# A latent-attention kernel: its preparation merged into one block, part of it beside the norms, and the steps behind its main loop re-ordered

## What is computed

```python
h = layernorm(layernorm(x)) * ln_scale + ln_bias        # the norms of two layers in a row
c_q, c_kv = h @ w_down_q.T, h @ w_down_kv.T             # 128 -> 64 each
q = rope(c_q @ w_up_q.T); k = rope(c_kv @ w_up_k.T)     # 16 heads of 64
v = c_kv @ w_up_v.T                                     # folded with w_out per head
attn = softmax(q @ k.T / 8)                             # 2048 x 2048 for each head
out = (attn @ v) @ w_out.T + 2 * x                      # the input comes in twice: here and around the layer
```

## Time and profile before

| | |
|---|---|
| median of 3 executions | 2093.56 us |
| the profiled execution's own time | 2090.94 us |
| its span, first to last instruction | 2089.1 us |
| PE busy over the span | 1881.3 us (90%) |
| DVE, ACT, POOL busy | 1605.3, 1259.2, 1076.7 us |
| mean granted TensorE clock | 0.950 of full speed |

### The profile page before, as it was taken

The page is one execution under the profiler, slowest core; times in us unless marked ns, Lnnn a source line. Parts: engine busy times, 40 slices in busy tenths (PEclk is TensorE's granted clock), DMA queues, the critical chain, the costliest instruction groups (busy, mean ns, idle before and its releaser), DMA issues. The chain is left out here.

```text
span 2089.1 us, 36118 instructions
## 1 busy us (share of the span) xinstructions
PE 1881.3 (90%) x11422; PEld 937.2 (45%) x11422; DVE 1605.3 (77%) x2448; ACT 1259.2 (60%) x2593; POOL 1076.7 (52%) x1225
## 2 busy tenths in 40 slices
PE   5755898989865999999999999999999999999598
PEld 2542486547642444444344443444443444444346
DVE  6787776676655788888888888788888888888265
ACT  6533685468520677777677777677776677777231
POOL 0735743574205466566566566566565566566200
PEclk9987899989976999999999999999999999999699
DMA  1001021002015699998898988899998889999243
GB/s 37 1 1 68 22 59 32 6 17 64 14 57 203 242 324 339 334 330 324 319 339 323 352 323 326 319 327 330 341 336 320 315 317 330 341 329 334 79 105 80
DMA packets 201467, 452.16 MB, mean 216 GB/s; under 512 B 12048, under 2 KB 159248, under 8 KB 200240
## 3 DMA queue, kind: packets, MB, share of 16 engines
q1 hardware_dynamic: 201264, 449.67, 60.9%
HBM read 228.77 MB, written 206.83 MB: 209 GB/s over the span
## 5 line engine op out<-in xcount | busy, mean ns | idle before, releaser
L1602 ACT ACTIVATE g.probs<-g_score,g.lowest 128x1024 f32<-128x1024 f32 x514 | 567.9, 1109 | 328.9 <-DVE g.lowest L1588 328.9
L1588 DVE TENSOR_REDUCE g.lowest<-g_score 128x1 f32<-128x1024 f32 x514 | 605.5, 1219 | 184.1 <-PE g_score L1556 184.1
L1556 PE MATMUL g_score<-g.keys,g.queries 64*128 64x512 f32 x2056 | 500.4, 605 | 20.5 <-PEq L1474 10.7
L1688 DVE STREAM_TRANSPOSE g.blocks<-g.probs 128x768 f32<-128x768 f32 x512 | 467.1, 950 | 1.0
L1618 PE MATMUL g_mix_ps<-g.far,mid.y_tok 128*64 128x512 f32 x1584 | 382.9, 605 | 0.0
L1556 PEld LDWEIGHTS g_score<-g.keys,g.queries 64*128 64x128 f32 x2056 | 183.7, 187 | 250.5 <-ACT g.probs L1602 130.8
L1648 POOL TENSOR_TENSOR g.scaled<-g.scaled,g.coef 128x1024 f32<-128x1024 f32 x67 | 127.0, 1896 | 247.8 <-ACT g.scaled L1640 240.0
L1708 POOL TENSOR_TENSOR mid.y_tok<-mid.y_tok,g.waves 128x512 f32<-128x512 f32 x128 | 162.3, 1268 | 76.0 <-ACT mid.y_tok L1571 76.0
L1461 POOL TENSOR_TENSOR g.queries<-mid.y_tok 64x256 f32<-64x256 f32 x256 | 185.4, 724 | 19.6
L1578 PEld LDWEIGHTS g_turned<-top.ident,g.probs 128*128 128x128 f32 x1024 | 107.6, 141 | 194.7 <-issue 194.7
L1578 PE MATMUL g_turned<-top.ident,g.probs 128*128 128x128 f32 x1024 | 168.4, 287 | 0.0
(11 more groups left out here) (369 smaller groups left out, 2778.7 us busy)
## 6 DMA issues: line engine op xcount, KB each, us to landing
g.far<-bounce SPq DMA_DIRECT2D x257, 768.0 KB, 7.0
bounce<-g.blocks SPq DMA_DIRECT2D x256, 768.0 KB, 6.2
e.share<-shares SPq DMA_DIRECT2D x8, 1024.0 KB, 16.9
g.far<-g.near SPq DMA_DIRECT2D x7, 768.0 KB, 6.7
lt0.v_late<-la0.v SPq DMA_DIRECT2D x6, 512.0 KB, 10.1
lt1.v_late<-la1.v SPq DMA_DIRECT2D x6, 512.0 KB, 9.4
bounce<-g.near SPq DMA_DIRECT2D x4, 768.0 KB, 9.4
top.upto<-stored_mixers SPq DMA_DIRECT2D x33, 64.0 KB, 6.5
```

Source lines behind the costliest of these rows:

```text
L1556: nc.tensor.matmul(score[:, 2 * pair + odd], queries[rows, turn, head, cols], keys[rows, turn, head, pair * CH:(pair + 1) * CH], start=Tru ...
L1588: nc.vector.tensor_reduce(lowest[:, unit, half, r:r + 1], score[:, 2 * half:2 * half + 2].rearrange("p b n -> p (b n)"), AX.X, ALU.max, ne ...
L1602: nc.scalar.activation(probs[:, r % 2, half * 2 * CH:(half + 1) * 2 * CH], score[:, 2 * half:2 * half + 2].rearrange("p b n -> p (b n)"), ...
L1688: ins = nc.vector.transpose(blocks[:, r, :, REST * half:REST * (half + 1)].rearrange("p j t c -> p t j c"), probs[:, r % 2, at:at + REST * ...
```

## The change

- `normalise_twice` now runs inside `latent_attention`, and its SP and POOL streams get work. SP issues all the loads of blocks 2 and 3, clears the retired semaphores, and, once POOL has zeroed `near`, issues the 11 fills of 768 KB. POOL does all the memsets.
- Blocks 2 and 3 become one. Small weights and the transposed tokens `hT` lie in unused halves of `queries`. ACT takes the transposed tokens, the lowered tokens and the values out of PSUM; scale, bias and factor ride on ACT's copy. PE computes the mixers first, then interleaves transposes, `lower` and the projections of the first chunks, with the values between the second and the third chunk.
- The rotary sums are split: DVE adds the keys of head 0, POOL the keys of head 1 and each head's queries once, and ACT copies the queries to the other half of the partitions (`cross`). The products have two buffers (`parts_of`), for alternate chunks.
- Behind the loop: PE does the output of the last unit but one ahead of the last mix; the last mix starts before the last `far` transfer has landed, with its columns split 384 and 128 (`mix_far`); and the last `add_output` moves from POOL to DVE.

The loop's own body is not changed. The diff, cut to its core:

```diff
-def normalise_twice(nc, x, cur, after):
+def normalise_twice(nc, x, cur, beside_sync, beside_pool):
...
-                after(sync)
+                beside_sync(sync)
+
+            @block.gpsimd
+            def _(pool):
+                beside_pool(pool)
...
-        normalise_twice(nc, x, cur, after=clear_retired)
...
+        hT = queries[:, 1, 0]
+        extra = queries[:, 1, 1]
+        w_down = extra[:, 0:2 * LATENT]
+        w_v = extra[:, 2 * LATENT:2 * LATENT + PAIRS_G * LATENT].rearrange("p (g n) -> p g n", n=LATENT)
+        w_o = extra[:, 640:640 + PAIRS_G * D].rearrange("p (g n) -> p g n", n=D)
+        norm = extra[:, 1664:1666]
+        by_rows = extra[:, 1666:1667]
+        parts_of = probs[:].rearrange("p a (b k n) -> p a b k n", b=2, k=2)
+
+        def load_front(sync):
+            for d, n in ((norm, "g_norm"), (w_down, "w_down")):
+                sync.dma_start(d, dram[n]).then_inc(m["front_loaded"], 16)
+            load_w(sync, 0, 0)
+            load_w(sync, 1, 1)
+            sync.dma_start(waves[:], dram["g_waves"]).then_inc(m["waves_loaded"], 16)
+            for d, n in ((w_v, "w_v"), (w_o, "w_o")):
+                sync.dma_start(d, dram[n]).then_inc(m["sides_set"], 16)
+            clear_retired(sync)
+            sync.wait_ge(m["zeroed"], 1)
+            for w in range(2):
+                for r in range(RT - w):
+                    sync.dma_start(far[:, w, 4 * r:4 * r + 4], near[:].rearrange("p a t n -> p (a t n)")
+                                   [:, 0:4 * RUN]).then_inc(landed[w], 16)
+            for r in range(RT):
+                sync.dma_start(bounce[4 + r].rearrange("(p x) -> p x", p=P), near[:].rearrange("p a t n -> p (a t n)")
+                               [:, 0:4 * RUN]).then_inc(written[r], 16)
+
+        def set_front(pool):
+            nc.gpsimd.memset(near[:], 0.0).then_inc(m["zeroed"], 1)
+            nc.gpsimd.memset(mixers[:, 0:2], 0.0)
+            nc.gpsimd.memset(mixed[:], 0.0)
+            nc.gpsimd.memset(coef[:], 1.0)
+            nc.gpsimd.memset(lowest[:], 0.0)
+            nc.gpsimd.memset(floor[:], 0.0)
+            nc.gpsimd.memset(sums[:], 1.0)
+
+        normalise_twice(nc, x, acc, load_front, set_front)
         with nc.Block() as block:
+            down_ps = (turned, mix_ps)
 
             @block.sync
             def _(sync):
-                load_w(sync, 0, 0)
-                load_w(sync, 1, 1)
+                sync.wait_ge(m["m_copied"], 4)
                 sync.dma_start(stored_mixers.rearrange("h p n -> p h n"), mixers).then_inc(m["mixers_stored"], 16)
+                sync.wait_ge(m["mixers_stored"], 16)
+                load_mixer(sync, 0, 1)
+                sync.wait_ge(m["v_copied"], 4)
                 for k in range(4):
                     sync.dma_start(values[k:P:4, NEAR:].rearrange("p t c -> p (t c)"), spread_values[32 * k:32 * k + 32])\
                         .then_inc(m["values_set"], 16)
                 sync.wait_ge(m["values_set"], 64)
-                sync.wait_ge(m["zeroed"], 1)
-                for w in range(2):
-                    for r in range(RT - w):
-                        sync.dma_start(far[:, w, 4 * r:4 * r + 4], near[:].rearrange("p a t n -> p (a t n)")
-                                       [:, 0:4 * RUN]).then_inc(landed[w], 16)
-                for r in range(RT):
-                    sync.dma_start(bounce[4 + r].rearrange("(p x) -> p x", p=P), near[:].rearrange("p a t n -> p (a t n)")
-                                   [:, 0:4 * RUN]).then_inc(written[r], 16)
-                sync.wait_ge(m["mixers_stored"], 16)
-                load_mixer(sync, 0, 1)
                 for w in range(2):
                     sync.wait_ge(landed[w], 64 - 16 * w)
                 for r in range(RT):
                     sync.wait_ge(written[r], 16)
+                sync.wait_ge(w_loaded[1], 16)
                 sync.wait_ge(mixer_loaded[0], 16)
+
+            @block.tensor
+            def _(pe):
+                def turn(g):
+                    if g >= 2:
+                        pe.wait_ge(m["hT_ready"], g - 1)
+                    for k in range(4):
+                        ins = nc.tensor.transpose(side[:, g % 2, k * P:(k + 1) * P], acc[:, 4 * g + k], ident[:])
+                    ins.then_inc(m["first_turned"], 1)
+
+                def lower(c_):
+                    pe.wait_ge(m["hT_ready"], c_ + 1)
+                    if c_ >= 2:
+                        pe.wait_ge(m["c_ready"], c_ - 1)
+                    nc.tensor.matmul(down_ps[c_ % 2][:], w_down, hT[:, c_ * CH:(c_ + 1) * CH], start=True,
+                                     stop=True).then_inc(m["down_done"], 1)
+
+                def first_pieces(c_):
+                    pe.wait_ge(m["c_ready"], c_ + 1)
+                    for swap in range(2):
+                        for kind in range(2):
+                            if c_ == 0:
+                                pe.wait_ge(m["m_copied"], 4)
+                            else:
+                                pe.wait_ge(m["first_free"], 4 * (c_ - 1) + 2 * swap + kind + 1)
+                            projected(score[:, 2 * swap + kind], 0, kind, swap, slice(c_ * CH, (c_ + 1) * CH))\
+                                .then_inc(m["first_full"], 1)
+
+                turn(0)
+                turn(1)
+                pe.wait_ge(m["sides_set"], 32)
+                for h in range(HEADS_G):
+                    rows = slice(h % 2 * 64, h % 2 * 64 + 64)
+                    at = h // 2 % 4
+                    for half in range(2):
+                        ins = nc.tensor.matmul(score[half * 64:half * 64 + 64, 2 * (h // 8) + h % 2, at * P:(at + 1) * P],
+                                               w_v[rows, h // 2], w_o[rows, h // 2], start=True, stop=True)
+                    if h % 8 == 7:
+                        ins.then_inc(m["m_done"], 1)
+                pe.wait_ge(m["front_loaded"], 32)
+                lower(0)
+                turn(2)
+                lower(1)
+                turn(3)
+                pe.wait_ge(w_loaded[0], 16)
+                first_pieces(0)
+                lower(2)
+                first_pieces(1)
+                lower(3)
+                pe.wait_ge(m["hT_ready"], NC)
+                for t in range(T):
+                    ins = nc.tensor.matmul(side[:, t // 8, (t % 8) * LATENT:(t % 8 + 1) * LATENT],
+                                           hT[:, t * P:(t + 1) * P], w_down[:, LATENT:], start=True, stop=True)
+                ins.then_inc(m["v_done"], 1)
+                first_pieces(2)
+                first_pieces(3)
+
+            @block.scalar
+            def _(act):
+                def take_turned(g):
+                    act.wait_ge(m["first_turned"], g + 1)
+                    nc.scalar.activation(hT[:, g * CH:(g + 1) * CH], side[:, g % 2], ACT.Identity, bias=norm[:, 1:2],
+                                         scale=norm[:, 0:1]).then_inc(m["hT_ready"], 1)
+
+                def take_lowered(c_):
+                    act.wait_ge(m["down_done"], c_ + 1)
+                    nc.scalar.activation(c[:, c_ * CH:(c_ + 1) * CH], down_ps[c_ % 2][:], ACT.Copy, scale=by_rows)\
+                        .then_inc(m["c_ready"], 1)
+
+                def cross(c_):
+                    act.wait_ge(m["q_placed"], 2 * c_ + 2)
+                    for head in range(2):
+                        nc.scalar.activation(queries[(1 - head) * 64:(1 - head) * 64 + 64, 0, head, c_ * CH:(c_ + 1) * CH],
+                                             queries[head * 64:head * 64 + 64, 0, head, c_ * CH:(c_ + 1) * CH], ACT.Copy)
+
+                act.wait_ge(m["front_loaded"], 32)
+                take_turned(0)
+                take_turned(1)
+                act.wait_ge(m["rows_set"], 2)
+                take_lowered(0)
+                take_turned(2)
+                take_lowered(1)
+                take_turned(3)
+                take_lowered(2)
+                cross(0)
+                take_lowered(3)
+                act.wait_ge(m["v_done"], 1)
...
+                cross(1)
+                cross(2)
+                cross(3)
 
+            @block.vector
+            def _(dve):
+                nc.vector.memset(by_rows[0:64], 0.125).then_inc(m["rows_set"], 1)
+                nc.vector.memset(by_rows[64:P], 1.0).then_inc(m["rows_set"], 1)
+                by_head = mixers[:, 2:].rearrange("p (g h) n -> p h g n", h=2)
+                for k in range(2):
+                    dve.wait_ge(m["m_done"], k + 1)
+                    for h in range(2):
+                        nc.vector.tensor_copy(by_head[:, h, 4 * k:4 * k + 4],
+                                              score[:, 2 * k + h].rearrange("p (g n) -> p g n", n=D)).then_inc(m["m_copied"], 1)
+                dve.wait_ge(m["first_turned"], NC)
+                nc.vector.tensor_scalar(acc[:], x[:], 2.0, None, ALU.mult).then_inc(m["doubled"], 1)
+                dve.wait_ge(m["waves_loaded"], 16)
+                for c_ in range(NC):
```

(55 more changed lines are left out.)

138 lines of the change are left out of this document (11 added, 127 removed).

## The result

The changed kernel takes 2057.26 us (median of 4 executions, 2055.98 to 2058.00) against 2094.26 us for the kernel before beside it (4 executions, 2087.83 to 2097.75): a ratio of 0.9826, with a 95% interval of 0.9802 to 0.9851. The forecast was 2055.0, the range 2046 to 2064.

The account below looks back on a forecast made before the run. PE fills the loop; ahead of it no engine is full and order costs. Gains of 27.0 us ahead of the loop and 11.8 behind sum to 38.8, taking the 2093.56 us median to 2055; range 2046 to 2064.

Parts of the forecast that it names:

- the front: Norms' start to the loop's first matmul: 51.9 us against 78.86, a gain of 27.0 us.
- the end: Behind the loop, to the last addition: a gain of 11.8 us.
- Part 1: Loads and fills beside the norms: SP is last at the barrier, and block 1 takes 21.5 us, 6.2 longer.
- rival B: Beside the norms: fills issue at 0.6 us each, the new block starts at 16 to 17 us, kernel 2048; chance 0.12.
- The loads behind the table: Beside the norms: `w_v` and `w_o`, queued behind the 2 MB table, may be held; two held issues of 3.9 us give 27.
- Part 2: Blocks 2 and 3 as one: POOL sets the pace, the block ends at T0+30.1, the loop starts 0.3 us later.
- the engine to watch: New block: ACT is new in it, with 16 copies, and might bring a wait no old row shows.
- the next limit: New block: values on PE precede the third chunk, which DVE has ready at 21.2, where POOL comes free at 21.4.
- The key sum on POOL: New block: moving one key sum to POOL gives 4.3 us a chunk against DVE's 4.84, worth some 2 us.
- Part 3: Behind the loop: last mix early and warm, last additions on DVE; the chain ends at 1950.5 against 1962.33.
- The loop: Loop's window: body unchanged, so 1245.7 us again, within 2.
- Rival E: In the loop: changed entry phase makes row steps wait for `far`; at 0.25 us each the kernel takes 2119; chance 0.03.

Follow-up runs that it names:

- e5: The changed kernel with SP issuing the 11 zero fills at the start of the new block, not beside the norms: 2055.68 us, ratio 0.9803.
- e6: The changed kernel with ACT's `cross` copies given back to POOL as two additions a chunk: 2059.17 us, one execution.
- e3: The changed kernel with 8 empty ACT instructions added ahead of the loop: 2053.60 us, ratio 0.9793.
- e7: The changed kernel with both key sums on DVE, leaving POOL two additions a chunk: 2057.37 us, one execution.
- e9: The changed kernel with all eight heads of the main loop written out, so no returns: 2038.93 us, ratio 0.9728.
- e10: The kernel before the change with all eight heads of the main loop written out, so no returns: 2079.80 us, ratio 0.9925.

## Why the prediction was right, and where it was wrong

**The total** was right, 2.3 us off, and partly by luck. In the profiles the front gained 3.6 us more than forecast and the end 0.8 more, while the loop took back 7.2 and the stages that nobody touched another 2.5: 5.3 us short in all. Of these, 3.3 are the profiled execution of before, which lay that far under its median.

**Part 1** was right in its mechanism, SP is late at the barrier, and wrong in one term. The price of a fill was taken as 1.2 us from the earlier trace rows, where it is issued behind other stores. Beside the norms an issue took 0.49 to 1.13 us, and the 11 cost 10.2. That price is not fixed, and the stores are not what sets it: in e5, with no store ahead of them, the fills took 13.9 us, and beside the norms the same stream took from 7.2 (e6) to 11.7 us (e3). What sets it is open. The first came where it was forecast, 6.9 us after the start of the block, behind 3.2 us of loads and 3.7 of clearing. The block comes to 17.5 us, not 21.5: 3.2 for the issues, and most of the 1.2 that was added on top. It lies between rival B (16 to 17) and the forecast; in e6 rival B's case came about, with the norms the last at 15.4 us. The loads behind the table were not held: 0.43 us each. POOL's memset cost DVE nothing (2.50 us for the four additions in the earlier trace rows and after). That the fills belong beside the norms was not borne out: they are as cheap in the new block (e5).

**Part 2** was right: 30.73 us against 30.4, with two terms off that cancel. ACT, named as the engine to watch, has 20 copies and not 16; its last ends at T0+30.2, together with POOL's last addition, where both were forecast (30 and 30.0). POOL's first addition came at T0+11.9 rather than 12.8, since the mixers took 3.47 us and not 3.7 and the first product started at T0+9.3, not 10.1. DVE's third chunk came late, by 0.6 us for POOL, since PE had the values before it. The forecast had named this as the next limit, and 0.2 us under it. The key sum on POOL was put at 2 us and is worth 0.7 (e7): POOL then has only two additions a chunk and DVE's 4.9 us replace POOL's 4.8, not 4.3. The 4.3 left out what the two engines do to each other. When DVE's key sum (two operands in SBUF) starts first, POOL's addition takes 1.69 us in place of 1.26. When POOL is first, as in e7, DVE's takes 1.67 in place of 0.68, as in the earlier trace rows. The Trainium skill (SBUF — State Buffer, section "Who interferes with whom") says that an instruction of DVE with two inputs in SBUF and one of POOL that reads SBUF contend, and that one of POOL that only writes does not. These rows agree with both halves. The Trainium skill's advice to keep additions of tiles on VectorE (GPSIMD Engine Reference, section 4.1) would cost 0.7 us here, by e7, a single profile.

**Part 3** was right, 14.55 us against 15.3. The 24 short instructions, which no row had shown, hide in L1665's 5.35 us together with the 384-column ones: the far mix costs in two pieces what it cost in one.

**The loop** is the step that failed: "in the loop's window 1245.7 us again, within 2". Rival E had the right place and the wrong mechanism. It looked at a phase between transfers and PE in 256 steps, and e9 and e10 exclude that to 0.04 us. The loss lies in three returns. They could be read in the trace of before: of the 10.3 us in which PE was idle over the loop, 9.75 were 2.58, 3.44 and 3.73 us at three places. I used that number as evidence that the loop was full and never asked where it lay.

## What to carry to other kernels

Ask of the idle time in a "full" loop where it lies: if it sits at the returns, it is the price of the jump, part of it can change with the length of the code ahead of the loop, and unrolling takes it away (here 18 us of 2057 with no other change). Before comparing two versions of a seam, compare the loop between them, since a gain of a few us can be masked by stalls of the same size that have nothing to do with it. Moving work out of a block into the shadow of another pays only as far as the engine that carries it isn't the last at the barrier.

## What the hardware showed that I had not expected

- A return of this loop stopped PE for 2.6 to 4.2 us, until 1.7 to 1.8 us after a packet of instructions had landed, and cost 2.7 to 7.6 us of the kernel's time. DVE, ACT and POOL stand still there too (3.3, 4.7 and 5.8 us at the first return of before).
- ACT may stall a second time just behind it, for 1.0 to 4.1 us, and 8 empty instructions ahead of the loop took the stall away.
- At or just behind 22 of the 28 returns profiled, PE's granted clock was at 0.5 (1.2 GHz) for 3.4 us, once for 6.8. In the main loops of e9 and e10, where PE stood for 0.58 us in all, it stayed at 1.00.
- The issue of 11 fills of 768 KB cost SP 7.2 to 11.7 us beside the norms, by the same stream, and 13.4 to 13.9 in the block of the loop's front (before and e5).
